# Waits of the attention that another wait implies are taken off TensorE, ScalarE and VectorE

## What is computed

```python
att = jnp.einsum('bhtd,bhsd->bhts', q, k) * scale + jnp.einsum('bhtd,tsd->bhts', q, rk)
att = jnp.where(causal[None, None], att, -jnp.inf)
att = jax.nn.softmax(att, axis=-1)
y = jnp.einsum('bhts,bhsd->bhtd', att, v) + jnp.einsum('bhts,tsd->bhtd', att, rv)
...
x = x + attn(_layernorm(x))
x = x + ffn(_layernorm(x))
```

## Time and profile before

| | us |
|---|---|
| median of 3 runs | 772.38 |
| lowest, highest | 769.88, 776.09 |
| profiled execution, span from first to last instruction | 770.0 |
| attention, about | 60 to 527 of the span |
| experts, about | 527 to 770 of the span |

### The profile page before, as it was taken

How to read it: one execution, slowest core, us unless ns; L and a number is a source line. 1 busy time by engine, 2 the same in 40 slices (tenths; PEclk the granted TensorE clock), 3 DMA queues, 4 the chain that set the end, 5 groups by cost and what they waited for, 6 DMA issues and landing times. The chain is left out here.

```text
span 770.0 us, 27094 instructions
## 1 busy us (share of the span) xinstructions
PE 690.5 (90%) x10316; PEld 507.9 (66%) x10368; DVE 589.2 (77%) x2036; ACT 514.7 (67%) x1032; POOL 255.8 (33%) x253
## 2 busy tenths in 40 slices
PE   4687879899888899988999988988999999999997
PEld 3465657677666677766777766766666666666665
DVE  7965686788787788787888887977566776677676
ACT  3686967688797878888888998887335343443331
POOL 9443445334355534545543445533000000000000
PEclk9988989999999999999999999999999999999999
DMA  9899998689989778787778779841000000000000
GB/s 255 262 295 335 333 303 264 203 244 277 309 250 302 255 222 253 249 238 241 236 222 266 221 232 255 271 153 50 3 22 28 29 5 23 28 15 1 14 15 14
DMA packets 117839, 138.48 MB, mean 180 GB/s; under 512 B 8976, under 2 KB 86288, under 8 KB 117520
## 3 DMA queue, kind: packets, MB, share of 16 engines
q1 hardware_dynamic: 117712, 136.75, 58.6%
HBM read 82.26 MB, written 54.46 MB: 178 GB/s over the span
## 5 line engine op out<-in xcount | busy, mean ns | idle before, releaser
L1075 DVE CUSTOM_DVE_ANT_0 ps<-ps,near 128x128 f32<-128x128 f32 (+3 forms) x512 | 245.1, 509 | 90.5 <-PE ps L837 57.0
L998 ACT ACTIVATE work<-ps,nmin 128x128 f32<-128x128 f32 (+3 forms) x512 | 248.4, 548 | 54.2 <-DVE nmin L1075 49.4
L849 PE MATMUL ps<-ident,work 128*128 128x128 f32 x1280 | 202.6, 278 | 20.7 <-issue 11.6
L849 PEld LDWEIGHTS ps<-ident,work 128*128 128x128 f32 x1280 | 157.0, 143 | 36.5 <-issue 13.7
L795 POOL TENSOR_SCALAR_AFFINE_SELECT work<-work 128x512 f32<-128x512 f32 x96 | 61.5, 641 | 237.8 <-ACT work L987 203.6
L1392 ACT ACTIVATE near<-ps 128x512 f32<-128x512 f32 x80 | 47.5, 595 | 133.3 <-PE ps L1357 133.2
L799 POOL TENSOR_TENSOR work<-work 128x512 f32<-128x512 f32 x96 | 124.2, 1294 | 8.0
L1060 DVE COPY work<-ps 128x512 f32<-128x512 f32 (+1 forms) x192 | 123.2, 642 | 2.5 <-issue 1.6
L837 PE MATMUL ps<-kb,qb 128*128 128x384 bf16 (+3 forms) x460 | 110.6, 298 | 12.3 <-ACT work L998 9.4
L1367 PEld LDWEIGHTS ps<-work,near 128*128 128x128 f32 x640 | 82.6, 192 | 34.2 <-issue 31.6
L987 ACT ACTIVATE work<-ps 128x512 f32<-128x512 f32 (+1 forms) x160 | 90.2, 564 | 18.7 <-PE ps L849 18.1
(11 more groups left out here) (111 smaller groups left out, 627.3 us busy)
## 6 DMA issues: line engine op xcount, KB each, us to landing
near<-w_slots SPq DMA_DIRECT2D x96, 512.0 KB, 5.4
w_slots<-relS SPq DMA_DIRECT2D x128, 256.0 KB, 4.5
qk_rows<-work SPq DMA_DIRECT2D x36, 256.0 KB, 4.7
near<-w_slots SPq DMA_DIRECT2D x32, 256.0 KB, 4.6
qk_rows<-y SPq DMA_DIRECT2D x9, 256.0 KB, 6.8
qb<-qk_rows SPq DMA_DIRECT2D x24, 96.0 KB
kb<-qk_rows SPq DMA_DIRECT2D x24, 96.0 KB
qb<-qk_rows SPq DMA_DIRECT2D x48, 48.0 KB
```

The lines of the kernel that those rows point to most:

```text
L849: ins = nc.tensor.transpose(tp_ps[:, m % 2, n * P:(n + 1) * P], prob[:, m % PROBS, n * P:(n + 1) * P], ident[:, :])
L998: ins = nc.scalar.activation(prob[:, m % PROBS, h * wide:(h + 1) * wide], qk_ps[:, m % 3, h * wide:(h + 1) * wide], ACT.Exp, bias=nmin[:, ...
L1075: nc.vector.tensor_tensor_reduce(out=scores, in0=scores, in1=near[:, q % NEAR, a, 4 * P - wide:4 * P, r], scale=1.0, scalar=3e38, op0=ALU. ...
```

## The change

No instruction that computes is added, removed or moved. Waits are taken out:

- `tp`: of the two copy counters only the one that counts unit `m - 2` is waited for, and `exp_done` only for the last three units (in the others `qk(m + 3)` stands ahead in TensorE's list and has waited for at least as much).
- `av`: no wait for its copies, but for the last two quads' units (`tp` of two units later stands ahead and has waited).
- `exp`: `min_done` alone, which thus moves onto the instruction; `tp_ready` is gone.
- `pT_copy`, by the new `wait_free`: `av_done` only where `av(q - 2)` doesn't stand early enough in TensorE's list, `pc_done` only for the first two units of a quad.
- `rel_copy`: the wait for the DMA out of its buffer (`w_out`) only where the reading of an earlier `near` doesn't already follow from the order.

```diff
+        def wait_free(engine, q, w, m):
+            if q >= 2 and SLOT_OF["av", q - 2] >= m + 3:
+                engine.wait_ge(av_done, q - 1)
+            if w < 2:
+                wait(engine, pc_done, q - 1)
...
                     if m >= 2:
-                        wait_copied(pe, m - 2)
-                    pe.wait_ge(exp_done, m + 1)
+                        pe.wait_ge(pTa_done if on_act(m - 2) else pTv_done, COPIES[on_act(m - 2)][m - 1])
+                    if m + 3 >= NU:
+                        pe.wait_ge(exp_done, m + 1)
...
-                    wait_copied(pe, last(q))
+                    if last(q) + 2 >= NU:
+                        wait_copied(pe, last(q))
...
-                    if q >= RSLOTS:
+                    if q >= RSLOTS and FIRST[q - RSLOTS] >= SLOT_OF["rel", q]:
                         k = q - RSLOTS
                         act.wait_ge(w_out[k % WSLOTS], 16 * (k // WSLOTS + 1))
...
-                    wait(act, av_done, q - 1)
-                    wait(act, pc_done, q - 1)
+                    wait_free(act, q, w, m)
...
-                    wait(act, tp_ready, m - PROBS + 1)
                     act.wait_ge(min_done, HEADS_BEFORE[m + 1])
...
-                    wait(dve, av_done, q - 1)
-                    wait(dve, pc_done, q - 1)
+                    wait_free(dve, q, w, m)
```

## The result

The change took 10.0 us off: 762.77 us (median of 4 runs, 761.69 to 764.67) against 772.76 for the kernel before beside it, a ratio of 0.9868 (95% interval 0.9828 to 0.9908). The forecast was 769.5, a gain of 2.9. (Ratios leave disturbed runs out, so one can differ from the quotient of two medians.)

A forecast was written before the change was run, and what follows sets the result against it. TensorE was taken as the attention's longest engine, with 44 us idle there, but not the only limit. Terms -0.6 - 0.2 - 2.1 = -2.9 us took the span from 770.0 to 767.1; plus 2.4 outside it, 769.5 us; range 762.5 to 776.5.

The forecast's parts named there:

- the likeliest case: Whole kernel: the forecast itself, a small gain that a measurement can hardly show; chance 0.50.
- the supply term: TensorE's instruction supply in the attention: fewer 256-instruction block edges in rv, 26 instead of 40, give -2.1 us.
- Exponentials, -0.6: ScalarE's exponentials: each that really waits starts 0.06 us sooner; ten counted, -0.6 us, at most 2.9.
- Copies, 0: pT copies and rel_copy: removed waits lie under other copies; 0, with 0.8 us as the far end.
- Transposes, -0.2: Before TensorE's transposes: 347 waits of 51 ns fewer, showing only where TensorE stands idle; -0.2 us, at most 1.9.
- av, 0: Before av on TensorE: 127 waits fewer, hidden under the transposes ahead; 0, or 6.5 us without that cover.
- the supply stalls go: Rival on TensorE: sequencer passes waiting transposes, reaches edges sooner, most of 23.1 us idle goes; 756 us, chance 0.10.
- Every wait on TensorE counts: Rival on TensorE: 474 waits of 51 ns fewer save 24.2 us in full, 748, or 760 half hidden; chance 0.07.
- edges in worse places: Rival on TensorE: delayed instruction packets fall on other edges, six more hit in full; slower, 781 us, chance 0.05.
- nothing reaches the end: Rival for the whole kernel: removed waits were satisfied early, edges trade places evenly; time stays 772.4 us, chance 0.28.
- the sign for the supply term: TensorE's breaks inside rv: the supply term is wrong if they don't move with the instruction list.
- the mark of failure: Attention: all wrong if TensorE's idle time falls over 8 us without rv's breaks as reason, or a new wait replaces them.

The follow-up runs named there:

- e3: The kernel before with 72 satisfied wait instructions more at the start of TensorE's list, moving block edges (15 in rv instead of 40); ratio to before 0.9936.
- e4: The changed kernel with 64 satisfied wait instructions more at the start of TensorE's list, moving block edges (42 in rv instead of 26); ratio to before 0.9856.
- e8: The kernel before with only the transposes' wait taken out of the exponentials on ScalarE, TensorE's list unchanged; ratio to before 1.0018.
- e5: The changed kernel with each of the 474 waits taken off TensorE replaced by a separate wait on counters already full; ratio to before 1.0010.
- e6: The changed kernel with two separate satisfied waits in each of the 474 places where TensorE lost a wait; ratio to before 1.0034.
- e7: The kernel before with only the 347 separate waits before transposes taken off TensorE; ratio to before 0.9933.
- e12: The kernel before with only the 127 separate waits before av taken off TensorE; ratio to before 0.9909.
- e9: The changed kernel measured again, in six runs; 766.00 us, ratio to before 0.9863.
- e1: The kernel before with only TensorE's 474 separate waits taken out, those of ScalarE and VectorE kept; ratio to before 0.9875.
- e2: The kernel before with only ScalarE's and VectorE's waits taken out, TensorE's list as before; ratio to before 0.9890.
- e11: The changed kernel with 75 of TensorE's 105 remaining separate attention waits put onto the last transposes of the unit ahead; ratio to before 0.9899.

## Why the prediction was right and wrong

The time came out inside the range, 0.3 us above its lower end; the likeliest case, a gain too small to tell, did not come. That it lies inside is luck: the range reached so low for other places of the edges (the supply term at -9), and e3 and e4 show that the places don't make the gain. The gain was over three times the forecast's, and the term at fault is *instruction supply*, -2.1 us.

*Exponentials, -0.6.* The release became 0.03 to 0.04 us as said. e8 puts the term between -1.3 and +4.1 us, so the value taken can't be told from nothing, and the far end of -2.9 is excluded. *Copies, 0*: no run shows a gain; e5, which has the exponentials' and the copies' edits together, allows 0.24% (1.9 us) at most. `rel_copy` is still seen waiting once for its DMA, 2.2 us.

*Transposes, -0.2, and av, 0.* Both were priced by the sequencer's 51 ns and found hidden. That part holds: e6 shows the 51 ns to be almost free. But e7 and e12 gained about 5 and 7 us, so the price was the wrong one. "The wait is hidden under the transposes ahead of it" is true of the gap in front of `av`, which is 0.17 us in both kernels; what the wait did was done up to a block's edge later. The comparison of the earlier trace rows looked at the instruction behind the wait, where nothing is to be seen.

*Supply, -2.1.* The prediction took 11.7 us x (1 - 26/40) = 4.1, and half of that. Three steps failed. First, that an edge outside `rv` costs nothing: in before, 17.9 us of pauses stand at edges, 5.4 of it outside `rv`, with 2.46 us in one go before transposes. Second, that the edges' places set the number of pauses: e3 and e4 moved them both ways, and it stayed. What sets it is how long before the edge the block is asked for, and separate waits delay that (e5). Third, the half: over the 14 profiles above, a straight line through spans and pauses gives 0.93 us of span for 1 us of pauses (correlation 0.80), though that alone doesn't say which is the cause. Measured, the pauses went from 17.9 to 6.7 us, and to 9.2 in e9: 9 to 11 us less, about the 10 gained. One profile by itself proves little: e1's has 14.8 us of pauses and e8's 13.3, and e1 gains where e8 doesn't. So that the whole gain goes through the pauses is likely, not shown. (The list of 21461 instructions also lacks 52 matmuls whose records are missing from the trace: each of the 10368 weight loads has one.)

By the Trainium skill (Runtime: NRT & Kernel Launch, "Instruction fetch mechanics") crossing an edge is mostly hidden. The trace agrees for some 56 of 70 edges before, and for 61 to 65 after; the others cost 0.4 to 2.8 us each, which that rule leaves out.

*The rival "the supply stalls go"* had the mechanism and got 0.10. It was argued down because "the longest breaks stand in `rv`, with no wait near". e5 shows that the wait needn't be near: it delays the request for a block that is used over 100 instructions later. Its 756 was too much by the price: it counted 11.4 us before transposes as supply, of which 3.3 stood at block edges, and took two thirds of 23.1 us, where 17.9 us stood at edges and 9 to 11 went. By the Trainium skill (Perfetto Trace Analysis, "Per-engine timelines") a sequencer-only instruction waits in the sequencer, while an engine's instruction waits in a queue behind it. The runs agree in that blocks are asked for sooner where separate waits are gone (188 and 174 instructions left against 156). e5 shows more than that rule says: a separate wait that is already satisfied isn't run either while an instruction ahead of it still waits, in none of 521 cases.

*Every wait on TensorE counts* falls with e6, *edges in worse places* and *nothing reaches the end* with the result, and e4, with 42 edges in `rv`, keeps the gain.

Of what was to be seen: exponentials at 0.03, 82 packets, `av` at 0.17 and few separate waits came as written. The idle time before `rv` fell to 4.4 instead of 8, and TensorE's waits for exponentials rose where they were to stay near 12 us (9.3 + 2.7 = 12.0 before `qk` then, 11.6 + 4.8 = 16.4 now). The breaks do move with the list, as the sign for the supply term asked: in all 14 profiles the pauses counted stand at the same place, give or take two instructions, in every 256. That sign couldn't tell what sets their number. That TensorE's idle time would fall by over 8 us was set as the mark of failure; it fell by 6.7, with the pauses at edges as the reason.

Open stay: why e3 gained 0.6% with pauses as before; whether ScalarE's and VectorE's edits are worth anything below 1.9 us; why e2's ratio is as low as 0.9890; and whether the whole gain goes through the pauses.

## What to carry to other kernels

In this kernel, on an engine with a long list of short instructions, a separate wait couldn't be priced by its own time or by the gap behind it: it kept the sequencer at the last instruction that still waited, and the bill came, as far as the traces show, as pauses at block edges, mostly in operations that have no wait at all. Count the idle pieces along the instruction list before explaining them by place. A wait that another implies is worth taking off such an engine even where it was always satisfied; putting it early onto an unrelated instruction may cost what it saves (e11, within its noise).

## What was not expected of the hardware

A pause can cost more than itself. After the 2.80 us up to 228.1 us in the changed kernel, TensorE's granted clock stands at 0.50 (1.2 of 2.4 GHz) from 228 to 234 us and is back at 1.00 by 236, in the windows above: 5.9 us of busy time at half the clock, up to 3 us more on top of the pause. In the kernel before, the 2.07 us at 137 us were followed by 0.50 as well (138 to 140 us), the 2.13 us of the earlier trace rows were not:

```profile
core 0: us, PE busy (x) PEld busy (x) DVE busy (x) ACT busy (x) POOL busy (x), PEclk, DMA share, GB/s
138.00:140.00 2.00, 1.82 (x20) 1.11 (x19) 0.76 (x2) 0.60 (x1) 0.05 (x1) 0.50 0.78 259
196.00:198.00 2.00, 1.01 (x25) 0.80 (x28) 0.40 (x1) 0.07 (x1) 0.55 (x1) 1.00 1.01 357
198.00:200.00 2.00, 2.00 (x64) 1.55 (x57) 1.26 (x6) 1.21 (x3) 0.00 (x0) 1.00 1.08 370
```

At rows 9's pause the clock is 1.00 in the 2 us that hold most of it and in the 2 us behind. So what one pause costs can't be told from its length alone.
